# Attention scores of two tiles at once on TensorE parts of 32 rows by 64 columns, placed between the probabilities' transposes and the projections

## The reference, cut to what matters

```python
# self-attention, 16 heads of 16, 4 groups of keys and values
scores = jnp.einsum('bhqd,bhkd->bhqk', q, k) * (1.0 / np.sqrt(d))
scores = jnp.where(causal[None, None, :, :], -jnp.inf, scores)
attn = jax.nn.softmax(scores, axis=-1)
out = jnp.einsum('bhqk,bhkd->bhqd', attn, v)
# cross-attention: the same without the mask; keys and values are the context's rows
scores = jnp.einsum('bghsd,bgtd->bghst', qh, kh) * scale
probs = jax.nn.softmax(scores, axis=-1)
out = jnp.einsum('bghst,bgtd->bghsd', probs, vh)
return out @ Wc.T + bc
```

## Time and profile before

| | |
|---|---|
| median of 3 executions | 809.72 us (807.61 to 810.27) |
| profiled execution | 804.97 us, its span 803.2 us |
| TensorE busy | 669.4 us, 83% of the span |
| VectorE, ScalarE, GpSimd busy | 479.0, 337.6, 351.2 us |
| attention phase | about 12 to 435 us of the span |
| mean granted TensorE clock | 0.91 |

### The profile page before, as it was taken

The page is one execution under the profiler, slowest core; times in us unless marked ns, Lnnn a source line. Parts: engine busy times, 40 slices in busy tenths (PEclk is TensorE's granted clock), DMA queues, the critical chain, the costliest instruction groups (busy, mean ns, idle before and its releaser), DMA issues. The chain is left out here.

```text
span 803.2 us, 16833 instructions
## 1 busy us (share of the span) xinstructions
PE 669.4 (83%) x6353; PEld 483.4 (60%) x6353; DVE 479.0 (60%) x1087; ACT 337.6 (42%) x636; POOL 351.2 (44%) x356
## 2 busy tenths in 40 slices
PE   1699999997899897889761899979999999987093
PEld 0366666665676665657530355557788789976072
DVE  3267776677788687777753899742333334433058
ACT  2477777766687576565521232211222222221000
POOL 5021122225444234243120383383777777757354
PEclk9899999999999899998965799989999999999555
DMA  7234444554533232231113500013999999994299
GB/s 229 26 58 82 82 81 82 101 96 89 111 71 66 48 71 57 35 60 35 33 40 93 184 0 1 0 49 106 233 237 252 242 239 252 275 254 62 29 320 314
DMA packets 112063, 94.26 MB, mean 117 GB/s; under 512 B 59760, under 2 KB 95856, under 8 KB 111984
## 3 DMA queue, kind: packets, MB, share of 16 engines
q1 hardware_dynamic: 96368, 74.57, 36.7%
q0 software_dynamic: 10240, 14.16, 9.5%
q10 hardware_dynamic: 5376, 4.46, 1.8%
HBM read 60.26 MB, written 24.50 MB: 106 GB/s over the span
## 5 line engine op out<-in xcount | busy, mean ns | idle before, releaser
L1230 POOL DMA_INDIRECT sum_d<-nz,targets x64 | 91.8, 1434 | 40.5 <-DMA sum_d<-nz,targets 11.9
L724 DVE TENSOR_REDUCE mx<-Sc 128x16 f32<-128x1024 f32 x64 | 77.8, 1216 | 33.4 <-PE Sc L401 33.2
L1057 PE MATMUL bank<-xnT,sgu_sb 128*128 128x512 f32 (+1 forms) x192 | 87.7, 606 | 11.7 <-PEq L1593 11.7
L1112 PE MATMUL bank<-xT,wgu_sb 128*88 128x96 f32 x1024 | 95.8, 247 | 0.3 <-ACT xT L1181 0.3
L1112 PEld LDWEIGHTS bank<-xT,wgu_sb 128*88 128x88 f32 x1024 | 90.0, 158 | 0.6 <-issue 0.5
L600 ACT COPY ET<-ring 128x512 f32<-128x512 f32 x128 | 69.3, 589 | 42.5 <-PE ring L413 40.4
L1281 DVE TENSOR_TENSOR hid<-sil,bank 88x192 f32<-88x192 f32 x64 | 22.4, 350 | 104.2 <-ACT sil L1187 104.2
L413 PE MATMUL ring<-ident,E 128*128 128x128 f32 x512 | 72.6, 286 | 14.3 <-ACT E L639 13.4
L429 PEld LDWEIGHTS O<-vbd,ET 128*64 128x64 f32 x2048 | 69.2, 142 | 25.1 <-issue 17.2
L728 DVE TENSOR_TENSOR E<-Sc,mx 128x1024 f32<-128x1024 f32 x64 | 78.4, 1225 | 6.9 <-DVE mx L724 0.5
L639 ACT ACTIVATE E<-E 128x1024 f32<-128x1024 f32 x64 | 67.5, 1055 | 29.7 <-DVE E L728 29.5
(11 more groups left out here) (152 smaller groups left out, 1139.0 us busy)
## 6 DMA issues: line engine op xcount, KB each, us to landing
wgu_sb<-in_wgu_dram SPq DMA_DIRECT2D x64, 352.0 KB
wd_sb<-in_wd_dram SPq DMA_DIRECT2D x64, 176.0 KB
sum_d<-zeros SPq DMA_DIRECT2D x16, 524.0 KB, 6.3
y<-sum_d SPq DMA_DIRECT2D x16, 512.0 KB, 8.8
kbd<-kT SPq DMA_DIRECT2D x248, 32.0 KB, 2.1
X<-in_x_dram SPq DMA_DIRECT2D x8, 512.0 KB, 6.5
rows_d<-xhT SPq DMA_DIRECT2D x8, 512.0 KB, 3.0
out_dram<-X ACTq DMA_DIRECT2D x8, 512.0 KB, 4.8
```

Of the source, the lines that this page charges most:

```text
L724: nc.vector.reduce_max(mx[:, m % 2, :], sc, AX.X).then_inc(s_mx, 1)
L1057: last = nc.tensor.matmul(out[0:m, :], sgu[:, e, k * MS + m0:k * MS + m0 + m], xnT[:, e, TOK * g:TOK * (g + 1)], start=e == 0, stop=e == 1)
L1112: last = nc.tensor.matmul(GP[e % 2][0:MH, CAP * u:CAP * (u + 1)], wgu[:, j, 4 * MH * c + MH * u:4 * MH * c + MH * (u + 1)], xT[:, e % 2, c ...
L1230: pool.indirect_dma_start(w["sums"][e % 2], bass.IndirectOffsetOnAxis(ap=targets[:, e:e + 1], axis=0), outs[:, e % EB, :], None, compute_o ...
```

## The change

Scores are made for two tiles (a pair) in one step, in even slots only. `Sc` becomes one tensor of four banks, with tile 2p in columns 0 to 255 and tile 2p+1 in columns 256 to 511 of every bank. A score matmul takes 32 rows (two heads) of `qT` and 128 columns of `kbd`, on one of eight parts of TensorE (four groups of rows by two of columns); the group of rows r writes bank r. A pair needs 32 such matmuls in place of 16 of 64 rows and 256 columns. The mask is written by 8 matmuls of 512 columns in place of 16 of 256. The step waits until both tiles of the last pair were subtracted (`s_sub` at 2p), where before one tile's buffer had to be free.

TensorE's slot m becomes: `pv` of m-1, `out_t` of m-2, `probs_t` of m, then in even slots the scores of tiles m+2 and m+3, `wc` of m-2, and the projections. `pv` moves from the end of the slot to its start. The other engines' order stays; waits for `s_sc` count pairs.

```diff
-                if m >= 2:
-                    pe.wait_ge(s_sub, m - 1)
-                for c in range(2):
-                    if not cross:
-                        for r, b in ((0, 0), (1, 0), (0, 1), (1, 1)):
-                            rows = slice(64 * r, 64 * (r + 1))
-                            nc.tensor.matmul(Sc[m % 2][64 * b:64 * (b + 1), r, 256 * c:256 * (c + 1)],
-                                             ident_bf[rows, rows], mask[rows, :], start=True, stop=False)
...
+                if p >= 1:
+                    pe.wait_ge(s_sub, 2 * p)
+                if not cross:
+                    for r in range(0, 4, 2):
+                        for k, b in ((0, 0), (1, 0), (0, 1), (1, 1)):
+                            rows = slice(64 * k, 64 * (k + 1))
+                            nc.tensor.matmul(Sc[64 * b:64 * (b + 1), r + k, :], ident_bf[rows, rows], mask[rows, :],
+                                             start=True, stop=False)
+                for n in range(2):
+                    for c in range(2):
+                        for b in range(2):
+                            at = 128 * (t + n) + 64 * b
+                            for r in range(4):
+                                rows = slice(32 * r, 32 * (r + 1))
+                                last = nc.tensor.matmul(
+                                    Sc[64 * b:64 * (b + 1), r, 256 * n + 128 * c:256 * n + 128 * (c + 1)],
+                                    qT[rows, g % 2, c, at:at + 64],
+                                    kbd[g % 2][rows, c, 2 * (t + n) + b, 2 * (r % 2):2 * (r % 2) + 2].rearrange(
+                                        "p h k -> p (h k)"), start=cross, stop=cross or (n == 1 and c == 1),
+                                    tile_position=(32 * r, 64 * b))
                 last.then_inc(s_sc, 1)
...
             for m in range(FIRST, LAST):
-                if 0 <= m + 1 < 2 * NT:
-                    scores(m + 1)
+                if 0 <= m - 1 < 2 * NT:
+                    pv(m - 1)
                 if crossed(m - 2):
                     out_t(m - 2)
                 if 0 <= m < 2 * NT:
                     probs_t(m)
+                if m % 2 == 0 and 0 <= m + 2 < 2 * NT:
+                    scores(m // 2 + 1)
                 if crossed(m - 2):
                     wc(m - 2)
...
-                if 0 <= m - 1 < 2 * NT:
-                    pv(m - 1)
...
             def shift(m):
-                dve.wait_ge(s_sc, m + 1)
-                sc = Sc[m % 2][:].rearrange("p r (h k) -> p (r h) k", k=S)
+                dve.wait_ge(s_sc, m // 2 + 1)
+                sc = Sc[:, :, 256 * (m % 2):256 * (m % 2 + 1)].rearrange("p r (h k) -> p r h k", k=S)
```

More of the change, by code:

```diff
@@ L104, in pair_of @@
 def pair_of(j):
-    r, c, m = j // 4, j // 2 % 2, j % 2
-    return 4 * c + 2 * r + m
+    r, c = j // 2, j % 2
+    return 4 * c + r
 def key_rows(g):
@@ L270, in block_keys @@
                 if g >= 2:
-                    sp.wait_ge(s_sc, 4 * (g - 1))
+                    sp.wait_ge(s_sc, 2 * (g - 1))
                 for c in range(1 if g == 0 else 2):
@@ L382, in values_t, with scores @@
                 last.then_inc(s_fill, 1)
-            def scores(m):
-                g, t = m // GT, m % GT
+            def scores(p):
+                g, t = 2 * p // GT, 2 * p % GT
                 cross = is_cross(g)
@@ L541, in xt @@
                     if v == 0:
-                        act.wait_ge(s_sc, 4 * (g - 1))
+                        act.wait_ge(s_sc, 2 * (g - 1))
                     nc.scalar.activation(qT[:, g % 2, :, cols].rearrange("p c (t q) -> p c t q", t=2), src,
@@ L727, in shift @@
                 dve.wait_ge(s_mx, m + 1)
-                nc.vector.tensor_tensor(E_[:, m % 2, :].rearrange("p (h k) -> p h k", k=S), sc,
-                                        mx[:, m % 2, :].unsqueeze(2).to_broadcast([128, H, S]),
+                nc.vector.tensor_tensor(E_[:, m % 2, :].rearrange("p (r h k) -> p r h k", r=4, k=S), sc,
+                                        mx[:, m % 2, :].rearrange("p (r h) -> p r h", r=4).unsqueeze(3).to_broadcast(
+                                            [128, 4, 4, S]),
                                         ALU.subtract).then_inc(s_sub, 1)
@@ L1474, in decoder_layer @@
         mem["ident_bf"] = sb("ident_bf", [128, 128], BF16)
-        mem["mask"] = sb("mask", [128, HQ * S], BF16)
+        mem["mask"] = sb("mask", [128, HH * S], BF16)
         mem["halfmask"] = sb("halfmask", [128, 2])
@@ L1502, in decoder_layer @@
         w["ctx2"] = sb("ctx2", [128, 2, GB, G * D])
-        mem["Sc"] = [pb(f"Sc{k}", [128, 2, 512]) for k in range(2)]
+        mem["Sc"] = pb("Sc", [128, 4, 512])
         mem["O"] = pb("O", [128, 512])
@@ L1530, in _ @@
                     nc.gpsimd.affine_select(out=m, in_=m, compare_op=ALU.is_ge, fill=MASKED,
-                                            base=0, pattern=[[0, HQ], [-1, S]],
+                                            base=0, pattern=[[0, HH], [-1, S]],
                                             channel_multiplier=1).then_inc(s_const, 1)
```

2 lines of the change are left out of this document (1 added, 1 removed).

## The result

The change made the kernel slower: 820.25 us, the median of four runs (818.2 to 822.35), against 808.71 on the same chip (807.61 to 810.27). The ratio is 1.0141, with an interval of 1.0107 to 1.0176. The forecast was 807.9 with a range up to 820. The profiled execution took 819.51, with a span of 817.8 (803.2 before).

A forecast was written before the change was run, and what follows sets the result against it. TensorE was taken to bound self-attention and VectorE's program the router's stage. Self-attention -0.5, keys +3.8, clock +3.5, router's stage -5.6 and tail -3.0 sum to -1.8 us, giving 807.9 us, range 800 to 820.

The forecast's parts named there:

- The pair block, 0.87 for 64 rows: TensorE's score matmuls: with eight parts side by side, a pair's 64 rows take 8 rounds, 0.87 us.
- rival (d): Score matmuls: only four of the eight parts work side by side, +0.86 per pair block, 829 us; chance 0.10.
- Self-attention and start, -0.5: Self-attention: -2.5 over five repetitions, +2 at the start, together -0.5 us, bounds -4 and +3.
- a gain of 0.5 for each of five repetitions: Self-attention: four slots take 20.25 us where they took 20.73, in all -2.5 us.
- The keys' loop, +3.8: Cross-attention groups 8 to 10: a loop through scores, wc, aggregation and key DMAs takes 23.4 us per four slots; +3.8 us.
- its clock, +3: Groups 8 to 10: three TensorE waits bring scores and wc at 1.2 GHz, +1 us each.
- The router's stage, -5.6: Cross-attention with the router: VectorE's waits for pv, 23.5 us, go and 17.9 us of new waits come; -5.6 us.
- 1.65, and 2.1 where there are no statistics: Router's stage, even slots from tile 43: VectorE's new wait for wc in us, ten slots, 17.9 in all.
- The tail, -3: After the last subtraction: waits of 1.61 and 2.36 us go but for about 1 us; -3 us.
- (a): Groups 8 to 10: the keys' loop doesn't bind, without +3.8 and +3.5 the time is 800.6 us; chance 0.20.
- (b): Whole attention: narrow scores save in full, 27.6 us, TensorE bounding all along; 782 us; chance 0.05.
- (c): Even slots: TensorE's new waits bring 1.2 GHz into the chain to the addition; 815 to 822 us; chance 0.25.

The follow-up runs named there:

- twelfth experiment: The changed kernel with pv issued twice in one of four self-attention slots, the output staying the same: 819.17 us, ratio 1.0152.
- fifth experiment: The changed kernel with the next group's statistics aggregation issued ahead of the addition that waits for wc on VectorE: 819.0 us, ratio 1.0165.
- first experiment: The changed kernel with wc of m-2 ahead of the pair's scores in even slots, nothing else: 792.73 us, ratio 0.9838.
- fourth experiment: The changed kernel with scores back at the head of odd slots and pv at the slot's end, pairs and narrow parts kept: 819.79 us, ratio 1.0162.
- eighth: The changed kernel with wc ahead of scores, exp between the copies of keys and values, and the statistics aggregation ahead of the addition: 783.5 us, ratio 0.9725.
- sixth: The changed kernel with pv put back to the slot's end, scores staying between the transposes and wc: 909.03 us, ratio 1.1289.
- third: The changed kernel in the same order, with score matmuls of 64 rows by 128 columns on four parts of TensorE: 848.59 us, ratio 1.0551.

## Why the prediction was wrong

The forecast summed to -1.8 us and the span shows +14.6. The 16.4 between them are, rounded, 9.4 in self-attention, 2.1 in the keys' groups, 5.2 in the router's stage and -0.4 in the tail. Step by step, as the prediction put them:

- **The pair block, 0.87 for 64 rows.** Eight parts side by side was right, rival (d) was wrong. The 0.87 is for the rounds alone; with its 0.1 for leaving the array the prediction had 0.97, and the block measures 1.14 to the next instruction. With the mask it is 1.70 in self-attention (1.53 forecast). It costs little where TensorE waits anyway. The estimate from the Trainium skill (TensorE: Matmul & The Clock Gate, Measured speedup vs the span model) was 1.13 for the rounds alone; the trace, 1.04 so counted, lies between it and 0.87.
- **Self-attention and start, -0.5: measured +8.9, the largest miss.** The wait for `exp` was right (2.0 forecast, 1.93 measured). What failed is, first, "a gain of 0.5 for each of five repetitions": four slots take 21.1, 0.4 more than 20.73, five times. The wait grew by 1.2 as forecast, but mask and scores save 1.4 in four slots and not 1.7, and the other rows didn't stay as they were: the transposes of the probabilities and the projections take 0.5 more in four slots. Why they do, no run shows. Second, "+2" at the start: the first `probs_t` waits 2.99 and starts at 44.06 (41.51 before), a spell follows, and tile 4 is at +5.5. Third, the clock was costed from tile 32 on only. "At full clock" holds for the kernel before; with the wait at 1.93 two more spells cost 1.5 each, one of them ahead of tile 24. That they come with this wait is shown by the twelfth experiment and the count there, though not every such wait has one.
- **The keys' loop, +3.8, and its clock, +3: measured +8.9 from tile 24's transposes to tile 43.** The waits stand where they were forecast, but they are 3.94, 1.97 and 1.51 us and not 4.5, 4 and 5.5: TensorE was less far ahead than forecast. Only the first has a spell right behind it (the mean clock of that stretch is 0.77, of the next two 1.00), so the clock's "+1 each" came true at one place of three. The second loop measures 23.0 (227.10 to 250.10; forecast 23.4), and group 11's scores (273.6) wait for the subtraction and no longer for `kbd`. The first is 20.6, from group 8's scores to group 9's, where 17.0 was expected: the spell behind the wait of 3.94 delays the context's transposes (212.05), and SP's first key DMA comes 6.1 us after `load_ctx`, not 2.9. The rest is not the loop. The fifth experiment opened it and got 0.9 us: the new wait for `wc` is there in these groups too (4.00, 2.03, 3.01 and 2.03 in the four even slots from 229 us on), and 1.5 are the second spell of self-attention. The prediction began to count that wait only at tile 43.
- **The router's stage, -5.6 and +0.5 for the clock: measured +0.1.** That 23.5 us of waits for `pv` go was right. What failed is the size of "1.65, and 2.1 where there are no statistics": it is 2.03 to 2.11, and 2.36 without. In the slot shown the scores take 1.13 and not 1.0, `wc` 1.13 and not 1.05, the addition starts 0.04 behind it, and the statistics cover 0.33 and not 0.45. The waits come to 24.5 instead of 17.9, with two spells in it (3.05 and 3.63).
- **The tail, -3: measured -3.4.** The number is right, in part by luck: by the last addition of `wc` (423.74, 410.23 before) it is -4.5, and 1.1 come back in the experts' part, which wasn't touched.
- **The rivals.** (a) and (b) are out. (c), slower through waits and 1.2 GHz at 815 to 822, has the time; its mechanism, the lower clock, is a part of the matter only. At full clock the router's stage would still be only some 2 us shorter than before, where 5.6 were forecast. What cancels the gain is the wait for `wc`: without it 3.0% go (first experiment, 1.0141 less 0.9838), some 25 us.

Two causes of the loss are shown by removing them: `wc` behind scores that wait for the subtraction (3.0% by itself), and `exp` behind the keys' and values' copies with one score block less in front (1.2% more, from 0.9838 to 0.9716). Not settled is the part from tile 31 to 43. It takes 61.95 us in the kernel before and 70.8 in the changed one, 63.6 with pairs in the old order (fourth experiment), and with narrow pairs and scores in the middle between 65.1 (eighth) and 78.7 (sixth). With the scores left in even slots no single edit to the changed kernel shortened it by more than 0.9: when one wait went, another or a spell took its place. Only once `wc` and `exp` had been moved did the aggregation's place count, from 69.6 to 65.1, in one execution of each.

## What to carry to other kernels

When a block of work is moved, list what stands behind it on its engine and who waits for that; a wait that was harmless at a slot's head costs its full length as soon as a result that another engine is waiting for is queued behind it. Putting `wc` in front of the scores moved two lines and brought 3.0%. Two edits, of which each alone loses or gives little (narrow parts in the old order 1.6% slower, the reordered pairs on wide parts 0.8% faster), were worth 2.8% with both, so the parts of a change should be timed apart and in both orders before it is dropped.

## What the hardware showed that I had not expected

With eight parts of 32 by 64, the first four rounds of eight follow each other every 0.11 us, about 14 ns for each row, and in the second half of the block a row starts only every 15 to 17 ns. What slows them no run shows. Narrowing from four wide parts to eight brought 1.96 to 1.14 us for the same products, a factor of 1.72.

A wait of TensorE was followed by 1.2 GHz in some cases and not in others of the same length. One of 1.68 us was and one of 2.80 wasn't. Waits of 1.93 us in self-attention were in two of six cases in the changed kernel, in none in the sixth experiment and in all six in the third; at 1.00 us (twelfth experiment) and 0.72 in none of this stage. The Trainium skill (TensorE: Matmul & The Clock Gate, The HAM clock gate) has idleness throttle the array to 1.2 GHz; the trace agrees in kind, but the same wait did and didn't do so, and with 1.06 us of useless work in place of a part of the wait none was left behind it. Where other engines wait for what TensorE runs at 1.2 GHz, one `pv` in another place made 40.3 us of four slots at a mean clock of 0.71, against 27.0 at 1.00 (sixth experiment); the waits that it added are in that number too.
